# ScalarE's copy of a finished group of values, put ahead of the current tile's exponent

## What is computed

```python
xn = layernorm(x, ln1_w, ln1_b)           # x: the context, (16, 1444, 128)
ln = layernorm(latents, ln2_w, ln2_b)     # latents: the tokens, (16, 100, 128)
q = ln @ Wq                               # 16 heads of 64
k, v = jnp.split(xn @ Wkv, 2, axis=-1)
q = q * (1.0 + scale[:, None, :, None]) + shift[:, None, :, None]
qk = jnp.einsum('bihd,bjhd->bhij', q, k) * attn_scale
attn = jax.nn.softmax(qk, axis=-1)
out = jnp.einsum('bhij,bjhd->bihd', attn, v).reshape(b, -1, INNER)
return out @ Wout
```

## Time and profile before

| | us |
|---|---|
| median of three runs | 1365.36 |
| lowest, highest run | 1363.19, 2264.54 |
| profiled execution | 1367.09 |
| its span | 1365.3 |
| `cross` in it, from the first scores to the last projection | 106 to 1050 |

### The profile page before, as it was taken

How to read it: one execution, slowest core, us unless ns; L and a number is a source line. 1 busy time by engine, 2 the same in 40 slices (tenths; PEclk the granted TensorE clock), 3 DMA queues, 4 the chain that set the end, 5 groups by cost and what they waited for, 6 DMA issues and landing times. The chain is left out here.

```text
span 1365.3 us, 32623 instructions
## 1 busy us (share of the span) xinstructions
PE 1152.9 (84%) x12753; PEld 905.5 (66%) x12758; DVE 1154.6 (85%) x2860; ACT 871.6 (64%) x1202; POOL 621.0 (45%) x512
## 2 busy tenths in 40 slices
PE   3567899999999999999999999999996548777778
PEld 2464677677776777767676776777775527776668
DVE  5886898998999899998999989988886278999984
ACT  0347778888888888887888788888874532122121
POOL 2354667565765657657576675657230000000000
PEclk9768899999999999999999999999998665676656
DMA  7017999999999999999999999999997200000000
GB/s 153 1 29 134 182 175 187 199 192 193 187 190 192 194 192 190 195 190 175 201 193 189 192 185 196 178 181 166 191 184 147 56 0 2 5 5 5 5 5 6
DMA packets 671122, 185.78 MB, mean 136 GB/s; under 512 B 655829, under 2 KB 668537, under 8 KB 670841
## 3 DMA queue, kind: packets, MB, share of 16 engines
q1 hardware_dynamic: 670968, 183.71, 79.3%
HBM read 19.51 MB, written 0.82 MB: 15 GB/s over the span
## 5 line engine op out<-in xcount | busy, mean ns | idle before, releaser
L1042 PE MATMUL ps<-pT,xa_hi 128*128 128x128 f16 x2288 | 386.4, 219 | 60.4 <-ACT uT L874 60.4
L851 ACT ACTIVATE e<-ps,bias 128x1444 f32<-128x1444 f32 (+1 forms) x208 | 305.5, 1469 | 171.8 <-DVE bias L923 171.4
L921 DVE TENSOR_REDUCE nmax<-ps 128x1 f32<-128x1444 f32 (+1 forms) x208 | 344.5, 1656 | 51.0 <-PE ps L1026 50.1
L1046 PE MATMUL ps<-pT,xa_hi 128*128 128x128 f16 x2288 | 386.6, 219 | 0.9 <-DMA pT<-p 0.9
L1043 PE MATMUL ps<-pT,xa_lo 128*128 128x128 f16 x2288 | 386.6, 219 | 0.0
L933 DVE TENSOR_TENSOR p<-e,p 128x1408 f16<-128x1408 f32 (+3 forms) x288 | 299.5, 1081 | 11.4 <-ACT p L859 8.5
L859 ACT ACTIVATE p<-e 128x1408 f16<-128x1408 f32 (+1 forms) x208 | 289.6, 1392 | 7.6
L1042 PEld LDWEIGHTS ps<-pT,xa_hi 128*128 128x128 f16 x2288 | 224.0, 99 | 91.7 <-issue 78.8
L811 POOL TENSOR_TENSOR p<-e,p 128x1408 f16<-128x1408 f32 (+1 forms) x128 | 196.6, 1557 | 183.7 <-ACT p L859 183.7
L1024 PE MATMUL ps<-xT_hi,q_hi 128*128 128x512 f16 (+1 forms) x624 | 229.5, 368 | 8.4 <-DMA xT_lo<-xa_lo 7.2
L1043 PEld LDWEIGHTS ps<-pT,xa_lo 128*128 128x128 f16 x2288 | 224.0, 99 | 12.2
(11 more groups left out here) (225 smaller groups left out, 1913.6 us busy)
## 6 DMA issues: line engine op xcount, KB each, us to landing
raw<-in_ctx SPq DMA_DIRECT2D x16, 704.0 KB
pT<-p SPq DMA_TRANSPOSE x416, 4.2
f_wq<-in_L_ffn_w_q SPq DMA_DIRECT2D x1, 1024.0 KB, 5.0
f_wqt<-in_ffn_wq_t SPq DMA_DIRECT2D x2, 512.0 KB, 7.1
raw<-in_ctx SPq DMA_DIRECT2D x48, 18.0 KB
x_tok<-in_x SPq DMA_DIRECT2D x1, 800.0 KB
out_x<-ost SPq DMA_DIRECT2D x6, 128.0 KB, 2.0
wk_t<-in_wk_t SPq DMA_DIRECT2D x1, 512.0 KB, 5.7
```

What stands on the lines that cost most here:

```text
L851: act.activation(e32[t % E_BUF][rows, :], score_banks(t)[rows, 0:T], ACT.Exp, bias=bias[rows, t % N_BUF:t % N_BUF + 1]).then_inc(e_done, 1)
L921: dve.tensor_reduce(nmax[rows, k:k + 1], score_banks(t)[rows, 0:T], AX_X, ALU.max, negate=True).then_inc(max_done, 1)
L1042: pe.matmul(out, hi, ph, start=n == 0, stop=False)
L1046: pe.matmul(out, hi, pl, start=False, stop=False)
```

## The change

In ACT's loop `take_values(v)`, which copies a finished group, now stands ahead of `exponent(t)`; nothing is added or removed, and the other engines' programs are the same.

```diff
             for t in range(ALL_TILES + DRAIN):
                 b, i = divmod(t, NM)
-                if t < ALL_TILES:
-                    exponent(t)
                 v = t - LAG
                 if 0 <= v < ALL_TILES and group_end(v):
                     take_values(v)
+                if t < ALL_TILES:
+                    exponent(t)
                 asked = [j for j in jobs_of(t) if j[0] == "q"]
```

## The result

| | us |
|---|---|
| changed kernel, median of four runs (lowest, highest) | 1342.49 (1340.84, 1345.50) |
| kernel before, median over the same comparison | 1364.62 |
| ratio, 95% interval | 0.9835 [0.9818, 0.9853] |
| profiled execution of the changed kernel; its span | 1341.98; 1340.2 |

What follows compares the result with a forecast made beforehand. DVE was taken to bound the kernel once PE stops waiting: 1.3 us per context over 15 steps, 19.5 us, plus 4.8 us of clock, off 1367.1, gave a median of 1342 us; 8 in 10 range 1316 to 1358.

Steps and rivals of the forecast that it cites:

- The copy earlier: ACT copies in iteration 7's 1.11 us idle time; PE gains 2.1 us there, at most 3.8 per context.
- The clock: Three contexts with PE at half clock after its idle time take 1.6 us more each; 4.8 us saved.
- The exponent later: ACT's exponent moves 0.48 us, its high half 0.19; iterations 2 and 11 pay at most 0.4 per context, counted 0.
- What DVE keeps waiting for: DVE's 1.10 us wait for tile 2's scores becomes a wait for ACT, leaving 2.1 of 3.2 us.
- A collision that the gain runs into: DVE's low half of tile 8 waits 0.8 us for POOL's L565, leaving 1.3 of 2.1 us.
- DMA: A faster PE eats into the transposes' slack; taken as 0, at most 0.3 us per context.
- The sum: 1.3 us per context over 15 steps, 19.5 us, plus 4.8 us for half-clock stretches: 1342 us.
- A: PE's wait is worth nearly its whole length, DVE giving all its 3.2 us per context: 1314 us; chance 0.14.
- B: DVE's waits for PE become waits for ACT and POOL; only 4.8 us of clock gained: 1362 us; chance 0.20.
- C: ACT's copy waits for its group's values, holding the exponent and what queues behind: slower, 1396 us; chance 0.06.
- D: The copy was late because of PE, not ACT's order, so moving it changes nothing: 1367 us; chance 0.02.

Runs made afterwards that it cites:

- e1: Kernel before with only iteration 7's copy moved ahead of the exponent, the other three left behind: 1344.04 us, ratio 0.9842.
- e2: Kernel before with the copies of iterations 11, 2 and 3 moved ahead of the exponent, iteration 7's left behind: 1365.56 us, ratio 1.0001.
- e7: Changed kernel with a second copy of each finished group, into a spare tile, ahead of the real one: 1351.51 us, ratio 0.9905.
- e4: Changed kernel with PE's low-half matmuls in `values` put behind all those with the high half: 1341.32 us, ratio 0.9822.
- e8: Kernel before with low halves of tiles 2, 3, 4, 6, 7 on POOL instead of 0, 3, 4, 7: 1350.96 us, ratio 0.9899.
- e5: Changed kernel with low halves of tiles 2, 3, 4, 6, 7 on POOL instead of 0, 3, 4, 7: 1335.05 us, ratio 0.9784.
- e3: Changed kernel with the first query job moved from iteration 1 to iteration 5: 1363.72 us, ratio 0.9984.

## Why the prediction was right

Point by point, by its steps:

- **The copy earlier: right.** PE's idle time in iteration 7 is gone, PE's wait is 8.2 us (under 20 was forecast), and e1 and e2 show that this copy carries nearly all of the gain.
- **The clock: right in kind.** The three stretches at a granted clock of 0.50 that the prediction counted, 3.4 us each, are absent; all contexts but the first stand at 1.00. In e2, where iteration 7's idle time stays, so do such stretches, five of them. 4.8 of the 20.5 us over the 14 steps are the clock's.
- **The exponent later, counted as 0: slightly wrong.** In e7 a high half that comes 0.48 us later in iteration 11 reaches DVE in full. The change itself delays it by 0.19 us there by the prediction's own sum, so an estimate of its price is 0.2 us per context, half of the 0.4 that the prediction allowed and set to 0. It named this as its way to be wrong in size.
- **What DVE keeps waiting for: right, to 0.01 us.** 1.10 + 0.32 us of waits in iteration 2 became 0.35 + 1.08. e2 shows the same exchange alone: 52.2 us of waits for 51.5, and no time.
- **A collision that the gain runs into: this step failed.** It took 0.8 us off the gain because the low half of tile 8 would wait for POOL's L565. It meets L565 as foreseen and is not held: 1.73 us. The mistake was to take the row of L602, a subtraction on 128x1536, for one of L565, a power on 128x12. The rows of before already had the right pair: the low half of the earlier trace rows started at 561.46, 0.11 us before L565 ended, and took its 1.73 us. The Trainium skill (SBUF — State Buffer, "Summary: rules for kernel authors") says that the second of two such instructions "fully blocks"; the row beside L602 (3.77 us) agrees with it, the row beside L565 does not. In place of the collision stand DVE's waits for ACT in iterations 10 to 12, 0.63 + 0.26 + 0.28 = 1.17 us per context: ACT runs from 605.32 to the end of the context without idle time, its exponents, queries and high halves set the pace there, and what DVE gained by PE's being early is partly given back. The 0.8 us taken off were thus the right kind of size for a wrong reason, and that the forecast came out within 1 us owes something to luck: without them the sum would have been 15 x 2.1 + 4.8 = 36 us instead of the 25.1 measured.
- **DMA, counted as 0: right.** Waits for transposes rose from 0.9 + 1.3 us to 16.7 + 24.0 (PE and its loads; the prediction's 1.3 is of the loads alone), and e4 shows that they cost nothing in this kernel.
- **The sum.** 24.3 us were forecast for the profiled execution and 25.1 came. Over the 14 steps 20.5 us came where 14 x 1.3 + 4.8 = 23.0 were forecast: the 1.3 us of the typical context came true, but not every context is typical (56.0 to 58.0), and the mean without the clock is 15.7 / 14 = 1.1 us. The first context made up for it, with 5.0 instead of 1.3 us, and that too is luck, since the prediction took it for one like the others. It is not: PE's wait before tile 4 was 4.52 us there, not 2.01, and is 0.66 now. These are PE's rows of that place before and after; then a window of before, in the columns of the earlier trace rows:

```profile
146.90 0.27 PE L1042 MATMUL ps<-pT,xa_hi 128*128 128x128 f16 x1 [4.52 <-ACT uT L874]
```

```profile
144.11 0.22 PE L1042 MATMUL ps<-pT,xa_hi 128*128 128x128 f16 x1 [0.66 <-ACT uT L874]
```

```profile
145.10:151.90 6.80, 5.00 (x41) 4.96 (x42) 4.04 (x17) 5.64 (x6) 3.80 (x3) 0.50 1.05 155
```

From within that wait on the granted clock was at 0.50 for 6.8 us; now it is at 0.50 for 3.4 us, at another place. At half the clock those 3.4 us saved are worth 1.7 us at most, an estimate; e8, which keeps the 4.52 us of wait but has only 3.4 us at 0.50 after it, is 1.8 us shorter in this context than before. How much of the 5.0 us each part brought, no run separates.

Of the rivals, A took DVE's 3.2 us as all to be had; DVE's waits fell by 1.0, the context by 1.3. The Trainium skill's rule beside it (Perfetto Trace Analysis, "Optimization Strategies"), that the matmul engine be kept busy, points to the right wait here; taken alone it overstates it: PE waited 52.2 us less for the copy and the time fell by 22. B is what e2 shows for three of the four copies. C did not occur in the changed kernel; its mechanism does in e5, which is faster all the same. D is excluded by e1.

## What to carry to other kernels

When two engines both need nearly the whole period, a wait of the one is worth only what the other can give up: add up busy time and waits of the second engine, take each of its waits apart, and ask who is late next behind it. Of several alike moves find the one place where the moved work fits into idle time of its own engine (here 1.11 us of ACT's); the other three places, moved by themselves, left the median where it was. Before a collision is booked, look for a row of the same pair of instructions at the same size. And before two gains are added or said to overlap, see whether both count the same stretches of a lower clock.

## What the runs showed of the hardware

- Not every two-input instruction of POOL holds DVE. Beside L602 (128x1536) DVE's low half took 3.77 us instead of 1.73, and in e3 DVE's L594 3.24 instead of 0.34. Beside L565 (128x12, 2.27 us long) it took its usual 1.73, also in e5, where the 128x1408 part of a low half at 542.18 lies wholly inside the L565 of 541.55 to 543.83. A long POOL instruction is not for that reason a blocking one. L565 differs from L602 in size and in operation, a power instead of a subtraction; no run tells which of the two matters.
- DVE instructions with one tile and scalars as inputs are held too: L965 took 0.96 us in e3 instead of 0.34, while POOL's L800 started at its side.
- PE at the lower of the two clock levels (granted 0.50, 1.2 GHz): in this stage each of the three stretches of 3.4 us in the repeated contexts of before followed PE's idle 2 us in iteration 7, but 11 other contexts had such idle time and no stretch. In e8, where PE's longest wait for the copy is 1.4 us, and in the changed kernel, where it is 0.7, none of the repeated contexts has one. No run here was aimed at what picks the three.
